# A perceiver layer on one core: time steps, score order and double buffers in the attention stage

## The reference, cut to what matters

```python
x = x + xattn(layernorm(x), ctx)        # 128 batches of 32 rows x 512; ctx 257 rows x 384; 16 heads of 32
#   scores = q @ k.T * scale; softmax over 257; out = probabilities @ v; then @ proj_w + proj_b
x = x + attn(layernorm(x))              # a delta rule, 32 time steps, 16 heads
#   S = S * a_t; delta = (v_t - k_t @ S) * beta_t; S = S + k_t (x) delta; y_t = q_t @ S
#   out = rmsnorm(y) * norm_w * silu(x @ Wg.T) @ Wo.T + bo;  k and q are normalised, beta = sigmoid(x @ Wb.T)
x = x + ffn(layernorm(x))               # 8 experts, the best 2 of each row
```

## Time and profile before

| | |
|---|---|
| median of 3 runs | 3549.56 us (3544.79 to 3549.81) |
| profiled execution, its own time | 3553.88 us |
| its span | 3552.1 us |
| PE busy | 3136.3 us (88%) |
| DVE busy | 2051.8 us (58%) |
| ACT busy | 1131.6 us (32%) |
| POOL busy | 988.6 us (28%) |

### The profile page before, as it was taken

How to read it: one execution, slowest core, us unless ns; L and a number is a source line. 1 busy time by engine, 2 the same in 40 slices (tenths; PEclk the granted TensorE clock), 3 DMA queues, 4 the chain that set the end, 5 groups by cost and what they waited for, 6 DMA issues and landing times. The chain is left out here.

```text
span 3552.1 us, 102137 instructions
## 1 busy us (share of the span) xinstructions
PE 3136.3 (88%) x42226; PEld 2298.2 (65%) x42226; DVE 2051.8 (58%) x4203; ACT 1131.6 (32%) x2656; POOL 988.6 (28%) x895
## 2 busy tenths in 40 slices
PE   7999999999998999999889999999999499888975
PEld 5777777766776777677667677776777356544542
DVE  2322456666666666666666666666666577793223
ACT  2333333333333333333333333333333133322221
POOL 2222222222222222222222222222221266600234
PEclk9999999999999999999999999999999788889997
DMA  4222222222222222222222222222221489535368
GB/s 155 84 85 72 89 77 75 74 91 78 80 74 91 77 74 74 91 77 81 79 98 78 74 88 81 74 79 91 78 78 54 124 231 264 172 122 148 122 227 308
DMA packets 297925, 379.11 MB, mean 107 GB/s; under 512 B 159568, under 2 KB 212304, under 8 KB 296016
## 3 DMA queue, kind: packets, MB, share of 16 engines
q1 hardware_dynamic: 287184, 338.19, 30.0%
q0 software_dynamic: 10240, 33.56, 2.8%
HBM read 258.17 MB, written 189.01 MB: 126 GB/s over the span
## 5 line engine op out<-in xcount | busy, mean ns | idle before, releaser
L117 PE MATMUL ring<-cond_high,wkv_high 128*128 128x342 f32 (+1 forms) x1152 | 406.4, 353 | 42.4 <-issue 21.0
L593 ACT ACTIVATE k_t<-ring,kvb 128x342 f32<-128x342 f32 (+1 forms) x384 | 209.4, 545 | 517.4 <-PE ring L117 517.3
L117 PE MATMUL ring<-cond_high,wkv_low 128*128 128x342 f32 (+1 forms) x1152 | 369.4, 321 | 0.0
L117 PE MATMUL ring<-cond_low,wkv_high 128*128 128x342 f32 (+1 forms) x1152 | 369.3, 321 | 0.0
L662 ACT ACTIVATE prob<-score,neg_max 128x257 f32<-128x257 f32 x512 | 235.9, 474 | 313.2 <-DVE neg_max L782 313.2
L117 PE MATMUL ring<-wkv_high,cond_high 128*128 128x512 f32 x768 | 320.1, 417 | 0.0
L170 DVE TENSOR_TENSOR prod<-prod 128x256 f32<-128x256 f32 (+5 forms) x352 | 303.8, 863 | 12.1
L166 DVE TENSOR_TENSOR prod<-coef,deltas 128x64 f32<-128x64 f32 (+30 forms) x248 | 303.9, 1226 | 4.9
L117 PE MATMUL ring<-wkv_high,cond_low 128*128 128x512 f32 x768 | 304.0, 396 | 1.8 <-issue 1.8
L117 PE MATMUL ring<-wkv_low,cond_high 128*128 128x512 f32 x768 | 304.4, 396 | 0.0
L117 PE MATMUL mix<-experts,xs_t 128*128 x624 | 296.5, 621 | 0.0
(11 more groups left out here) (199 smaller groups left out, 5885.6 us busy)
## 6 DMA issues: line engine op xcount, KB each, us to landing
cond<-cond_t_dram SPq DMA_DIRECT2D x128, 385.5 KB, 3.9
xs<-slot_rows SPq DMA_DIRECT2D x78, 256.0 KB
slot_rows<-ys SPq DMA_DIRECT2D x78, 256.0 KB
x_rows<-x SPq DMA_DIRECT2D x64, 256.0 KB, 2.9
vb_rows<-vgb SPq DMA_DIRECT2D x64, 256.0 KB, 3.2
x_in<-x_dram SPq DMA_DIRECT2D x32, 256.0 KB, 4.6
v_last_s<-v_last_rows SPq DMA_DIRECT2D x512, 0.5 KB
kk_rows<-kk_rows_s SPq DMA_DIRECT2D x32, 256.0 KB, 2.6
```

The costliest lines, as they stand in the source:

```text
L117: last = pe.matmul(out, lhs_t, rhs, start=(i == 0), stop=(i == len(terms) - 1))
L593: act.activation(k_t[:, group, at:at + n], ring_bank[bank][:, 0:n], ACT.Identity, bias=kvb[:, group:group + 1]).then_inc(ring.free[bank], 1)
```

## The change

Nine edits in `first_pass`:

- The tiles of probabilities and of values are doubled (`prob`, `v_s`); to make room, `xn` lies in `x_in`, `x1n` in `q_s`, and `kq` in the second probability tile.
- PE makes `scores(1)` before it turns batch 0, and `scores(b+1)` after `attend(b-1)`; values of a batch come before the attend of the one ahead. The waits on `exp_done` guard the score tile.
- The product `GT`, its sigmoid on ACT, its two POOL products (`gate_rows`) and its store move from the middle of the turn to its end (the store to the next turn); the order of the ring's lists follows.
- `V2`'s last chunk waits for `grams_read`, where `QT` did.
- DVE's time steps stand in six places (`CUTS`): after the row statistics; after `spread_decays`; after `read_grams`; and in each of batches 1 to 3 after `normalise(b)`. None is left between `q_s` and `maximum(0)`.
- The quarters are divided anew: 13, 8, 6 and 5 steps for 13, 7, 6 and 6.
- `move_turned(b-1)` comes after `maximum(b)`, `move_attended(b-1)` after the steps.
- The residual is made before the rows are normalised in place, both after the first steps.
- On SP, `load_x`, the value rows and conditions of batches 2 and 3 are issued before the wait for the steps.

```diff
-STEPS = ((0, 13), (13, 20), (20, 26), (26, 32))
+STEPS = ((0, 13), (13, 21), (21, 27), (27, 32))
+CUTS = ((0, 5, 8, 10, 11, 12, 13), (13, 15, 17, 18, 19, 20, 21), (21, 23, 24, 25, 26, 27, 27), (27, 28, 29, 30, 31, 32, 32))
...
     BOTH = ["K00", "K01", "K02", "K03", "K10", "X1T", "K11", "K12", "KK", "QQ", "K13", "XT", "LD", "K20", "K21",
-            "BT", "GT", "K22", "K23", "QT", "V2", "V00", "V01"] + A[16:]
-    B = ["X1T", "KK", "QQ", "LD", "BT", "GT", "V2"]
+            "BT", "K22", "K23", "QT", "V2", "V00", "V01", "L0", "V10", "V11", "O0", "L1", "V20", "V21", "O1",
+            "L2", "V30", "V31", "O2", "L3", "GT", "O3", "PR"]
+    B = ["X1T", "KK", "QQ", "LD", "BT", "V2", "GT"]
+    A = [name for name in BOTH if name not in ("X1T", "KK", "QQ", "LD", "BT", "V2", "GT")]
...
-        xn = sb("xn", [P, D])
+        xn = x_in
         xn_t = sb("xn_t", [P, DC, P])
         q_s = sb("q_s", [P, HG, P])
+        x1n = q_s[:].rearrange("p g t -> p (g t)")
         k_t = sb("k_t", [P, HG, MU])
-        v_s = sb("v_s", [P, 2, D])
+        v_s = sb("v_s", [P, 2, 2, D])
         v_last = sb("v_last_s", [P, 2, HG, P])
-        prob = sb("prob", [P, HG, M])
+        prob = sb("prob", [P, 2, HG, M])
+        kq = prob[:, 1].rearrange("p g m -> p (g m)")[:, 0:HG * BU * 2 * N].rearrange("p (i t) -> p i t", t=2 * N)
...
+                    ring.wait_full(sp, "XT", u - 1)
...
+            def store_gate(u):
                 sp.wait_ge(gate_ready, u)
-                sp.dma_start(rows["gate"][v, :], vgb[:, 1, :]).then_inc(gate_stored, 16)
+                sp.dma_start(rows["gate"][unit_rows(u - 1), :], vgb[:, 1, :]).then_inc(gate_stored, 16)
...
+                if not last:
+                    more = not (isinstance(u, int) and u == NU - 1)
+                    if more:
+                        load_x(u + 1)
+                    load_v_last(u, 2)
+                    if more:
+                        load_cond(u + 1, 2)
+                    load_v_last(u, 3)
+                    if more:
+                        load_cond(u + 1, 3)
                 if group is not None:
                     first, end = STEPS[quarter]
                     sp.wait_ge(steps_done, group * N + end)
...
+            def gate_rows(u):
+                pool.wait_ge(silu_ready, u)
+                own.then(pool.tensor_tensor(vgb[:, 1], vgb[:, 1], steps_of[:].rearrange("p h t -> p (h t)"), ALU.mult))
+                pool.tensor_tensor(by_head(1), by_head(1), normw[:].unsqueeze(1).to_broadcast([P, H, HD]), ALU.mult)\
+                    .then_inc(gate_ready, 1)
...
+                gate_rows(u)
...
+            def exponentials(u, b):
+                act.wait_ge(neg_max_ready, u * BU + b + 1)
+                for g in range(HG):
+                    act.activation(prob[:, b % 2, g, :], score[:, g, 0:M], ACT.Exp, bias=neg_max[:, g:g + 1],
+                                   accum_out=sums[:, g:g + 1]).then_inc(exp_done, 1)
+
+            def move_turned(u, b):
+                act.wait_ge(turned_ready, u * BU + b + 1)
+                act.activation(prob_t[:, 0, :], turned[0][:], ACT.Copy).then_inc(prob_t0_ready, 1)
...
-                    wait_stored(gate_stored, u)
-                    sigmoid("GT", u, steps_of[:].rearrange("p h t -> p (h t)"), copy=vgb[:, 1, :]).then_inc(silu_ready, 1)
...
                     for b in range(BU):
-                        n = u * BU + b
-                        act.wait_ge(neg_max_ready, n + 1)
-                        for g in range(HG):
-                            act.activation(prob[:, g, :], score[:, g, 0:M], ACT.Exp, bias=neg_max[:, g:g + 1],
-                                           accum_out=sums[:, g:g + 1]).then_inc(exp_done, 1)
-                        move(f"V{b}0", u, v_s[:, 0, :])
-                        move(f"V{b}1", u, v_s[:, 1, :])
-                        act.wait_ge(turned_ready, n + 1)
-                        act.activation(prob_t[:, 0, :], turned[0][:], ACT.Copy).then_inc(prob_t0_ready, 1)
+                        exponentials(u, b)
+                        if b > 0:
+                            move_turned(u, b - 1)
+                        move(f"V{b}0", u, v_s[:, b % 2, 0, :])
+                        move(f"V{b}1", u, v_s[:, b % 2, 1, :])
+                    move_turned(u, BU - 1)
+                if b_:
+                    wait_stored(gate_stored, u)
+                    sigmoid("GT", u, steps_of[:].rearrange("p h t -> p (h t)"), copy=vgb[:, 1, :]).then_inc(silu_ready, 1)
...
+                def some_steps(place):
+                    if group is not None:
+                        steps(group, quarter, CUTS[quarter][place], CUTS[quarter][place + 1])
 
                 if not last:
                     dve.wait_ge(x_loaded, 16 * u + 16)
-                    norm_rows(x_in[:], 0, 2 * u + 1, xn[:]).then_inc(xn_ready, 1)
-                if group is not None:
-                    steps(group, quarter, cut[0], cut[1])
+                    statistics(x_in[:], 0)
+                some_steps(0)
+                if not last:
+                    residual(u)
+                    normalised(x_in[:], 0, 2 * u + 1, xn[:]).then_inc(xn_ready, 1)
                 if not first:
                     log_decays(u)
                     spread_decays(u)
-                if group is not None:
-                    steps(group, quarter, cut[1], cut[2])
+                some_steps(1)
                 if not first:
                     read_grams(u)
-                if not last:
-                    residual(u)
-                if group is not None:
-                    steps(group, quarter, cut[2], cut[4] if last else cut[3])
+                some_steps(2)
                 if last:
+                    for place in range(3, 6):
+                        some_steps(place)
                     return
 
                 bank = ring.wait_full(dve, "QT", u)
                 dve.scalar_tensor_tensor(q_s[:], ring_bank[bank][:].rearrange("p (g t) -> p g t", g=HG), SCALE,
                                          qb_scaled[:].unsqueeze(2).to_broadcast([P, HG, P]), ALU.mult, ALU.add)\
                     .then_inc(ring.free[bank], 1)
-                if group is not None:
-                    steps(group, quarter, cut[3], cut[4])
...
                 maximum(0)
                 normalise(0)
-                move_turned(0)
                 for b in range(1, BU):
                     maximum(b)
+                    move_turned(b - 1)
+                    normalise(b)
+                    some_steps(2 + b)
                     move_attended(b - 1)
-                    normalise(b)
-                    move_turned(b)
+                move_turned(BU - 1)
                 move_attended(BU - 1)
 
                 bank = ring.wait_full(dve, "PR", u)
                 dve.tensor_tensor(x1[:], ring_bank[bank][:], x1[:], ALU.add).then_inc(ring.free[bank], 1)
                 ring.wait_read(dve, "PR", u)
-                norm_rows(x1[:], 1, 2 * u + 2, x1n[:]).then_inc(x1n_ready, 1)
+                statistics(x1[:], 1)
+                normalised(x1[:], 1, 2 * u + 2, x1n[:]).then_inc(x1n_ready, 1)
...
-                products(pe, bank[:], terms).then_inc(full, 1)
+                products(pe, bank[:], terms[:-1], stop=False)
+                if (b, j) == (0, 1):
+                    pe.wait_ge(exp_done, (u * BU + 1) * HG)
+                products(pe, bank[:], terms[-1:], start=False).then_inc(full, 1)
...
+                if b + 2 < BU:
+                    pe.wait_ge(exp_done, (n + 2) * HG)
                 pe.wait_ge(prob_t0_ready, n + 1)
                 pe.wait_ge(prob_t1_ready, n + 1)
-                ring.wait_read(pe, f"V{b}1", u)
                 pe.wait_ge(v_last_loaded[b % 2], (u * 2 + b // 2) * 64 + 64)
-                ring.wait_read(pe, f"L{b}", u)
+                if b == BU - 1:
...
-                    by_token("GT", u, x1n_t, wattn[:, 3])
                 if a:
                     keys(u, 2, 2)
                     keys(u, 2, 3)
                     ring.wait_read(pe, "XT", u)
-                    if b_:
-                        pe.wait_ge(grams_read, u)
                     by_channel("QT", u, wq, xn_t)
                 if b_:
                     bank, full = bank_of("V2", u)
                     for c in range(DC):
                         if a and c == DC - 1:
+                            pe.wait_ge(grams_read, u)
                             ring.wait_read(pe, "K23", u)
                             ring.wait_read(pe, "QT", u)
                         ins = pe.matmul(bank[:], x1n_t[:, c, :], wattn[:, 2, c, :], start=(c == 0), stop=(c == DC - 1))
...
                     scores(0)
                     values(u, 0, 0)
                     values(u, 0, 1)
+                    scores(1)
                     turn_probabilities(u, 0)
                     for b in range(1, BU):
-                        scores(b)
-                        attend(u, b - 1)
                         values(u, b, 0)
```

(57 more changed lines are left out.)

8 lines of the change are left out of this document (1 added, 7 removed).

## The result

The change makes the kernel slower: 3617.6 us median of 4 runs (3613.7 to 3623.0) against 3548.2, a ratio of 1.0195, 95% interval 1.018 to 1.021. The profiled execution took 3613.7 us (before: 3553.9), its span is 3611.9.

What follows compares the result with a forecast made beforehand. PE was taken to bound the first pass, its one wait there being for scaled probabilities (107.8 us). 3553.9 + 84 for units with steps - 15.5 (units without, last turn) = 3622 profiled, 3618 median; range 3585 to 3650.

Steps and rivals of the forecast that it cites:

- the units with steps: The 27 first-pass units with time steps and attention: mean attention part 39.5 against 36.4, +3.1 us each, +84 us.
- the last turn: End of the first pass, where PE waits for deltas: runs steps 27 to 31, no longer 26, so -5 us.
- The chain and the claims: Batches: DVE's 5.0 us plus step and c against PE's 7.3 delays the banks V20, V30 and GT claim.
- The collision c: POOL's condition split lengthens each step in the batches: 1.7 us in quarter 0, 2.1 in the others.
- the full block: Rival, 15%: DVE waits out both POOL instructions at each batch step, c = 2.55, slow clock fully exposed; about 3670.
- its line: DVE step lengths from t=20 (4.12 us) and t=26 (5.05): 0.155 us more a step.
- The slow clock: PE runs slowly after its last stop of 3 to 5 us: 0.7 us added in quarter 0, 1.4 elsewhere.
- The sum: Start times of V20, V30, GT and projection per quarter; attention parts without GT 35.55, 40.35, 37.9, 39.4 before slow clock.
- Units without steps: Five units with attention alone: PE's saving taken nearly whole, 2.1 us each, -10.5 us.
- What was costed at nothing: Delays taken as covered: residual and normalised rows, `V2`'s gram wait, SP's order, GT's sigmoid and POOL products, shared buffers.
- The decoupling wins: Rival, 17%: POOL and DVE overlap in the batch steps without delay, c = 0; about 3478 profiled, 3475 median.
- doesn't do what it says: Rival, 8%: some wait on SP or the ring binds first, attention part stays near 36.4; 3553.9 less 15.5.

Runs made afterwards that it cites:

- e2: Changed kernel with `move_attended(b-1)` ahead of its batch's time steps instead of behind them: 3702.2 us, ratio 1.043.
- e1: POOL's split cut to one column per batch from unit 2 on, in both kernels: changed kernel 3483.7 us (0.981), kernel before 3518.8 us (0.991).
- e3: Changed kernel with the old quarters and step places, last steps again between `q_s` and `maximum(0)`: 3500.1 us, ratio 0.986.
- e4: Kernel before with the change's quarters, steps in four places where DVE is idle, and SP's loads ahead of its wait: 3436.6 us, ratio 0.968.
- e6: Changed kernel, no steps in the batches, most late steps ahead of `q_s`, only 12 and 20 before the projection's addition: 3383.2 us, ratio 0.952.
- e5: Changed kernel with no steps in the batches, the last ones between the last move and the projection's addition: 3419.2 us, ratio 0.963.

## Why the prediction was right

Predicted 3618, measured 3617.6. The mechanism was right: each step delays a move that frees the bank PE claims next, and POOL's split lengthens the steps. That the number agrees within 0.4 us is luck, because three parts of the sum were off and cancel: +84 for the units with steps came to +78.5 (72.5 and 6.0), -10.5 for those without to -13.4, and -5 for the last turn to +5.4. The sum of the parts was +68.5, and they measured +70.5.

- **The chain and the claims: right.** The prediction had V20 at 15.1, 16.7, 17.8, 18.55 in the four quarters; measured 14.9, 16.7, 17.7, 18.4. V30 at 24.55, 27.75, 29.95, 31.45; measured 23.6, 26.7 to 27.5, 29.5, 31.0. GT in quarters 0 and 1 at 34.15 and 38.95; measured 32.5 and 37.7. The moved wait of e2, 3702 in a range of 3690 to 3710, comes from the same chain.
- **The collision c: right in kind, too large in size.** 1.7 and 2.1 were taken, a mean of 2.0; e1 against the changed kernel gives 1.7, and 1.2 instead of 1.7 in quarter 0. In step 25 it is 1.95 us, beside a cast and a subtraction of 0.83 and 1.65 us alone; no kind of step reached the 2.55 of the full block, the case that the Trainium skill's rule was read to give ("SBUF — State Buffer", Who interferes with whom). The rows of step 25 show what is hidden: each instruction that has waited ends about 0.15 us sooner after the other's end than its length without a wait. The first fold ends 0.81 us after the cast (0.96 in e1), the subtraction 1.50 after the first fold (1.65 in the earlier trace rows), the second fold 0.41 after the subtraction (0.56 in e1). That the one waits to the other's end agrees with the rule.
- **What the rows of before already held.** The split met not only maxima, copies and idle time there but also 20 first scalings (e1's kernel before). And beside the single row of 1.35 us the prediction took the steps' lengths from steps 20 and 26, which met no POOL product. In the same trace POOL's gate products met steps 10, 18, 24 and 30 of every group, and these took 3.95, 5.77, 7.28 and 7.54 us (medians), 1.3 to 2.5 over its line; step 18 runs from 1587.97 to 1593.75 (its folds and the first of the products are below). So the collision was on record there in size, in the front part, beside other POOL work. Steps 10, 18 and 30 got no longer by moving into the batches (3.97, 5.80, 7.56); the other seven kinds there grew by 0.4 to 2.0 us, and a bank of PE now waits for each.

```profile
1589.36 3.12 DVE L170 TENSOR_TENSOR prod<-prod 128x576 f32<-128x576 f32 x2
...
1588.02 2.43 POOL L555 TENSOR_TENSOR vgb<-vgb,steps_of 128x512 f32<-128x512 f32 x1 [2.39 <-ACT steps_of L619]
```

- **The slow clock: too small in quarters 0 and 1.** 0.7 and 1.4 were added. Against a unit without steps, GT to projection took 1.7 us more in quarters 0 and 1, V30 to projection 1.3 and 1.5 in quarters 2 and 3. The last stops were 2.2, 4.25, 2.8 and 3.6 us, not 3 to 5, and the shortest cost as much as the longest. e3, expected from the same view ("too short"), missed by 63 us, mostly for this reason. (The page's digit 9, read as 0.9, stands for 90% or more: the granted clock was 0.97.)
- **The sum:** attention parts of 39.85, 45.35, 42.9 and 44.4 (with the 3.6 of GT back in) against 39.2, 44.4, 42.6 and 44.2. +3.1 a unit was forecast, +2.8 came over units 5 to 30. The profile's own total, forecast 3622, was 3613.7, the lowest of the four runs and with a second pass 10.6 us shorter than before's.
- **Units without steps:** -2.1 each forecast, -2.7 measured. **Last turn: wrong.** -5 was forecast because it has one step less. It took 5.4 more, because three of its steps stand behind `read_grams`, and its last step ends 54.3 us after the last projection instead of 49.2. **What was costed at nothing:** the front part fell to 47.2 where 46.7 stood, so those covers held but for half a microsecond.
- **The rivals.** "The decoupling wins" named c as what decides: with c taken away, 3483.7 for the 3475 it had (its four projections give a mean of 33.9, not 34.2, so about 3468). The change loses because of POOL, not because of the order. "The full block" and "doesn't do what it says" did not occur.

Two points were beyond the prediction. It treated the order and the steps' places as one trade, but they are separable: the places (e4, with the new quarters and SP's earlier loads, which were not tried apart) are worth 113 us and the rest of the change on top of them 17 to 42, while the steps inside the batches cost about 200 us against the same kernel with the steps elsewhere (3617.6 against 3419.2). And even with c = 0 the batches stay a bad place, since a step of 3.8 us or more does not fit between DVE's 5.0 and PE's 7.3: e1's changed kernel is 100 us behind e6.

## What to carry to other kernels

Work that fills idle time of an engine has to be put where that engine's chain is not the one that frees the next buffer: count the chain's time per stage, with the move behind the filler, against the stage's length on the bound engine, before moving anything. A low busy share (DVE 58%) said that room existed, not where; the idle time before the grams was free until it was full (quarter 2 of e6), that in the batches was not. Look at what the neighbour on a shared resource does in the new place: here a split that had met no time step cost more than the reordering won. And look for steps that the neighbour lengthens already in the old profile: they give the price.

## What was not expected of the hardware

- Stops of 2.2 to 3.8 us of PE were enough for the slow level. Behind the 2.22 us of quarter 0 at GT the clock was 0.56 for 3.41 us (window in the section on the result), behind the 3.75 us of e3 0.56 for 7.0 us, and behind the 2.44 us of e5 0.76 in the mean of 7.1 us (row below). The 1.09 us stop at V30 of unit 18 was followed by 3.46 us at 1.00. The expectation of e3 had taken 2.3 us as too short.

```profile
1405.90:1413.00 7.10, 7.06 (x35) 7.06 (x36) 1.64 (x5) 1.64 (x3) 0.56 (x1) 0.76 0.72 260
```

- Both sides lose in a collision. The gate's two POOL products took 2.02 and 2.08 us beside a time step in e5, where they take 1.26 to 1.28 in units without steps, while the step itself took 7.6 us for 5.7. The kernel before shows it too: 2.43 and 1.67 us beside its step 18.
